# Criss-cross attention on one core: value projection in units of 512 positions instead of 384

## What is computed

```python
q = einsum('oc,bchw->bohw', Wq, x) + bq          # 64 channels, k alike
v = einsum('oc,bchw->bohw', Wv, x) + bv          # 512 channels
energy_H = einsum('bchw,bcgw->bhwg', q, k) - NEG * eye   # along the column of a position
energy_W = einsum('bchw,bchv->bhwv', q, k)               # along its row
att = softmax(concatenate([energy_H, energy_W], -1), -1)
out = gamma * (v summed with att along column and row) + x
```

## Time and profile before

| | |
|---|---|
| median of three runs | 3735.42 us (3734.54 to 3739.78) |
| span of the profiled execution | 3739.5 us (the highest of the three runs is 3739.78 us) |
| PE busy | 3683.0 us, 98% of the span |
| DVE, ACT, POOL busy | 72%, 41%, 17% |
| DMA queue q1 | 869.67 MB, 75.9% of 16 engines |
| PE's share of the chain that ended last | 96% |

### The profile page before, as it was taken

The page is one execution under the profiler, slowest core; times in us unless marked ns, Lnnn a source line. Parts: engine busy times, 40 slices in busy tenths (PEclk is TensorE's granted clock), DMA queues, the critical chain, the costliest instruction groups (busy, mean ns, idle before and its releaser), DMA issues.

```text
span 3739.5 us, 67129 instructions
## 1 busy us (share of the span) xinstructions
PE 3683.0 (98%) x26968; PEld 3663.5 (98%) x26968; DVE 2674.2 (72%) x4324; ACT 1533.3 (41%) x2130; POOL 649.6 (17%) x816
## 2 busy tenths in 40 slices
PE   8799999999999999999999999999999999999999
PEld 7799999999999999999999999999999999999999
DVE  8767787677876778767786677866778657786555
ACT  7523444244442445424454244542444424444111
POOL 1410023100331003210042000420004200042000
PEclk9899999999999999999999999999999999999999
DMA  8687768877698776977769777697776977769665
GB/s 268 178 230 254 254 215 234 245 253 248 203 246 247 240 256 191 259 237 254 247 190 255 242 245 254 196 251 240 259 232 204 250 229 255 230 210 254 204 211 180
DMA packets 333956, 873.97 MB, mean 234 GB/s; under 512 B 34640, under 2 KB 186704, under 8 KB 333648
## 3 DMA queue, kind: packets, MB, share of 16 engines
q1 hardware_dynamic: 333648, 869.67, 75.9%
HBM read 661.92 MB, written 207.62 MB: 233 GB/s over the span
## 4 chain that ended last, share of the span: by engine, by line
PE 96%; DVE 3%; DMA 1%; issue 0%; ACT 0%; SPq 0%; POOL 0%; DVEq 0%; POOLq 0%
PE bank L1044 43%; PE bank L1011 19%; PE bank L1032 18%; PE bank L960 10%; PE bank L972 3%; PE bank L981 3%; DVE E L735 1%; PE bank L996 0%; DVE Sx L714 0%; DVE Sx_first L714 0%; DMA XT_r<-in_x_row 0%; DVE mx_c L730 0%; DVE mx_r L730 0%; DVE zs_c L745 0%; DMA XA_first<-in_x 0%
## 5 line engine op out<-in xcount | busy, mean ns | idle before, releaser
L1044 PE MATMUL bank<-Sy,Wv_hi 128*128 128x384 f32 x6144 | 1595.3, 340 | 8.6 <-DVE Sy L719 8.6
L1044 PEld LDWEIGHTS bank<-Sy,Wv_hi 128*128 128x128 f32 x6144 | 1089.0, 189 | 9.8 <-DVE Y L809 9.8
L1044 PE MATMUL bank<-Sy,Wv_lo 128*128 128x384 f32 x3072 | 1028.5, 335 | 0.0
L809 DVE SCALAR_TENSOR_TENSOR Y<-bank,bv_sb,Y 128x384 f32<-128x384 f32 x768 | 470.3, 612 | 723.9 <-PE bank L1044 723.1
L1032 PE MATMUL bank<-Pt,XT_r 128*128 128x96 f32 x6144 | 719.3, 275 | 3.7 <-DMA XT_r<-in_x_row 3.7
L1032 PEld LDWEIGHTS bank<-Pt,XT_r 128*128 128x128 f32 x6144 | 715.9, 192 | 4.4 <-DMA XT_r<-in_x_row 4.1
L484 POOL TENSOR_TENSOR Pe<-Pe,F 128x384 f32<-128x384 f32 x336 | 286.0, 853 | 2389.5 <-DMA Pe<-e_scratch 2351.0
L617 ACT ACTIVATE Sy<-Y 128x768 fp32r<-128x768 f32 x384 | 319.0, 842 | 793.4 <-PE bank L1044 747.3
L1044 PEld LDWEIGHTS bank<-Sy,Wv_lo 128*128 128x128 f32 x3072 | 577.4, 188 | 0.0
L605 ACT ACTIVATE Y<-bank 128x384 f32<-128x384 f32 x384 | 326.9, 851 | 429.3 <-PE bank L1011 429.3
L793 DVE COPY Y<-bank 128x384 f32<-128x384 f32 x384 | 317.7, 827 | 214.5 <-PE bank L1011 198.0
(11 more groups left out here) (73 smaller groups left out, 3030.2 us busy)
## 6 DMA issues: line engine op xcount, KB each, us to landing
XT_r<-in_x_row SPq DMA_DIRECT2D x384, 384.0 KB, 6.0
Y<-in_x SPq DMA_DIRECT2D x192, 768.0 KB, 5.5
out<-Y SPq DMA_DIRECT2D x184, 768.0 KB, 4.2
XA<-in_x SPq DMA_DIRECT2D x180, 768.0 KB, 6.4
XT_r<-in_x_col SPq DMA_DIRECT2D x192, 384.0 KB, 8.2
XT_c<-in_x_col SPq DMA_DIRECT2D x192, 384.0 KB, 8.0
e_scratch<-E SPq DMA_DIRECT2D x384, 144.0 KB, 3.0
Pe<-e_scratch SPq DMA_DIRECT2D x336, 144.0 KB, 7.6
```

The source lines that it names most:

```text
L809: nc.vector.scalar_tensor_tensor(at, proj_ps[c % 2][:, 0:CP], bv_sb[:, c:c + 1], at, op0=ALU.add, op1=ALU.add).then_inc(out_made, 1)
L1044: last = nc.tensor.matmul(proj_ps[c % 2][:, 0:CP], w[:, ct, at], Sy[:, lo, ct, :], start=(ct == 0 and k == 0), stop=(ct == CT - 1 and k == 2))
```

## The change

Projection no longer follows chunks. The 9216 positions are cut into 18 units of 512 (`UNIT`), each projected with matmuls of 512 columns. A unit covers parts of two chunks, so rounding, `low_y` and `finish` are made in two pieces (`pieces(u)`); three units cover four chunks. After the four slots of a unit PE attends the 5 or 6 image rows of unit u + 2 in one burst (`rows_of`), and 11 rows stand ahead of the first unit where 8 stood. There is a second place for energies behind the slots: slot 4 lies behind the burst's first three rows, slot 5 behind its end. `A_SLOTS` puts three chunks of keys and queries into each of units 5 to 12, `B_SLOTS` the 24 column groups into units 12 to 16. Outputs lie two slots behind the sums (`SPARE`), `Y` has 26 slots, and the last two chunks are stored in quarters. The scratch for software DMA is given as 2048.

```diff
+UNIT = 512
+UNITS = POS // UNIT
+SPARE = 2
+BANKED = CHUNKS - SPARE
+def rows_until(u):
+    return -(-UNIT * (u + 1) // N)
+A_FIRST, A_LAST = 5, 12
+A_SLOTS = {5: (1, 3, 4), **{u: (0, 2, 4) for u in range(6, A_LAST + 1)}}
+B_SLOTS = {12: (5,), **{u: range(6) for u in range(13, 16)}, 16: (0, 1, 2, 3, 4)}
+AFTER_TILES = 4
...
-        Y = sb("Y", [P, CHUNKS + 1, CT, CP])
+        Y = sb("Y", [P, CHUNKS + SPARE, CT, CP])
-        Sy = sb("Sy", [P, 2, CT, CP], F32R)
+        Sy = sb("Sy", [P, 2, CT, UNIT], F32R)
...
             def row_stage(b, more):            # SP
-                load_xtr(b, 3)
+                load_xtr(b, RRING)
+                load_xtr(b, RRING + 1)
                 load_xres(b, 0)
-                load_xtr(b, 4)
-                load_p(b, CHUNKS + 4)
-                load_xtr(b, 5)
+                load_xtr(b, RRING + 2)
+                load_xres(b, 1)
+                load_p(b, CHUNKS + PRING + 1)
+                load_p(b, CHUNKS + PRING + 2)
+                load_freed_xtr(b, 1)
...
+            def round_y(b, u):                 # ACT; low_y and finish on DVE alike
+                act.wait_ge(r_added, past(r_added, b * N + rows_until(u)))
...
+                    for n, lo, at, width in pieces(u):
+                        last = nc.scalar.activation(Sy[:, 0, cts, at:at + width], Y[:, n + SPARE, cts, lo:lo + width], ACT.Copy)
+                    last.then_inc(y_hi_made, 1)
...
+                    def after(slot):           # ACT, row_stage
+                        m, x_next, g = kq(u, slot), split(u, slot), group(u, slot)
+                        if x_next is not None:
+                            round_x(b + 1, x_next, 0)
+                        if m is not None:
+                            evict_kq(b + 1, m)
+                        if x_next is not None:
+                            round_x(b + 1, x_next, 1)
+                        if m is not None:
+                            exponentials(b + 1, m)
+                        if g == 0:
+                            gather_q(b + 1, 0)
+                            gather_q(b + 1, 1)
+                        if g is not None:
+                            if g + 2 < CHUNKS:
+                                gather_q(b + 1, g + 2)
+                            exponentials(b + 1, CHUNKS + g)
+                    for c in range(CT - 1):
+                        after(c)
+                    if group(u, CT - 1) is None:
+                        after(CT - 1)
+                    if u + 1 < UNITS:
+                        round_y(b, u + 1)
+                    if group(u, CT - 1) is not None:
+                        after(CT - 1)
+                    after(AFTER_TILES)
+                    after(AFTER_TILES + 1)
...
+                    for c in range(CT):        # DVE, row_stage
+                        low_x_after(c)
+                        finish(b, u, c)
+                        shift_after(c)
+                        if c and kq(u, c - 1) is not None:
+                            sum_z(b + 1, kq(u, c - 1))
...
+                    rows = rows_of(u + 2)
+                    for h in range(HALVES):
+                        if u + 1 < UNITS:
+                            low_y(b, u + 1, h)
+                        for i in rows[h:h + 1]:
+                            add_row(b, i)
+                    low_x_after(AFTER_TILES)
+                    for i in rows[2:3]:
+                        add_row(b, i)
+                    shift_after(AFTER_TILES)
+                    for i in rows[3:]:
+                        add_row(b, i)
...
-                        last = nc.tensor.matmul(proj_ps[c % 2][:, 0:CP], w[:, ct, at], Sy[:, lo, ct, :],
+                        last = nc.tensor.matmul(proj_ps[c % 2][:, :], w[:, ct, at], Sy[:, lo, ct, :],
...
+                for i in range(rows_until(1)): # PE, row_stage
+                    attend_row(b, i)
...
+                    for c in range(CT):
+                        if kq(u, c) is not None:
+                            project_kq(b + 1, kq(u, c))
+                        project(b, u, c)
+                        energies_after(c)
...
+                    if kq(u, AFTER_TILES) is not None:
+                        project_kq(b + 1, kq(u, AFTER_TILES))
+                    rows = rows_of(u + 2)
+                    for i in rows[:3]:
+                        attend_row(b, i)
+                    energies_after(AFTER_TILES)
+                    for i in rows[3:]:
+                        attend_row(b, i)
+                    energies_after(AFTER_TILES + 1)
```

More of the change, by code:

```diff
@@ L30, with rows_of, turned_for, pieces @@
 COPIES = P // BLOCK
-A_FIRST, A_LAST = 6, 17
-B_FIRST, B_LAST = 18, 22
-B_EACH = 5
-def a_chunks(n):
-    return [2 * (n - A_FIRST), 2 * (n - A_FIRST) + 1] if A_FIRST <= n <= A_LAST else []
-def b_groups(n):
-    first = (n - B_FIRST) * B_EACH
-    return list(range(first, min(first + B_EACH, CHUNKS))) if B_FIRST <= n <= B_LAST else []
+UNIT = 512
[4 more added lines that the diff above has]
+    return -(-UNIT * (u + 1) // N)
+def rows_of(u):
+    return range(rows_until(u - 1), rows_until(u)) if u < UNITS else range(0)
+def turned_for(u):
+    return [i // ROWS for i in rows_of(u) if i % ROWS == 0]
+def pieces(u):
+    at, out = 0, []
+    while at < UNIT:
+        n, lo = divmod(u * UNIT + at, CP)
+        width = min(CP - lo, UNIT - at)
+        out.append((n, lo, at, width))
+        at += width
+    return out
+def first_unit(n):
+    return n * CP // UNIT
+def last_unit(n):
+    return ((n + 1) * CP - 1) // UNIT
+A_FIRST, A_LAST = 5, 12
+A_SLOTS = {5: (1, 3, 4), **{u: (0, 2, 4) for u in range(6, A_LAST + 1)}}
+B_SLOTS = {12: (5,), **{u: range(6) for u in range(13, 16)}, 16: (0, 1, 2, 3, 4)}
+AFTER_TILES = 4
+def kq_chunk(u, slot):
+    slots = A_SLOTS.get(u, ())
+    return (u - A_FIRST) * 3 + slots.index(slot) if slot in slots else None
+def split_chunk(u, slot):
+    if (u, slot) == (A_FIRST - 1, AFTER_TILES):
+        return 0
+    m = kq_chunk(u, slot)
+    return m + 1 if m is not None and m + 1 < CHUNKS else None
+def column_group(u, slot):
+    slots = list(B_SLOTS.get(u, ()))
+    return sum(len(B_SLOTS[v]) for v in B_SLOTS if v < u) + slots.index(slot) if slot in slots else None
 def out_slot(n):
-    return n % (CHUNKS - 1)
+    return n % BANKED
 def criss_cross_attention(nc, x, x_col, x_row, wqk_t, wv_t, bqk, bv, gamma, out):
@@ new lines, in row_stage @@
+                load_p(b, CHUNKS + PRING + 2)
+                load_freed_xtr(b, 1)
+                for u in range(UNITS):
+                    kq, split, group = stage_plan(more)
+                    if kq(u - 1, AFTER_TILES) is not None:
+                        store_row_energies(b + 1, kq(u - 1, AFTER_TILES))
+                    for n in range(CHUNKS):
+                        if first_unit(n) == u + 1:
+                            load_xres(b, n)
+                    if more and u == A_FIRST - 1:
@@ new lines, in row_stage @@
+                    if more and u == UNITS - 1:
+                        load_p(b + 1, PRING)
+                    for c in range(CT):
+                        if split(u, c) is not None and split(u, c) + 2 < CHUNKS:
+                            load_xa(b + 1, split(u, c) + 2)
+                        if kq(u, c) is not None:
+                            store_row_energies(b + 1, kq(u, c))
+                        if c < CT - 1 and group(u, c) is not None:
+                            store_column_energies(b + 1, group(u, c))
+                        if c == 1:
+                            for n in turned_for(u + 2):
+                                if n + PRING < CHUNKS:
+                                    load_p(b, CHUNKS + n + PRING)
@@ L403, in row_stage @@
+                    if u < UNITS - 1:
+                        for n in range(BANKED):
+                            if last_unit(n) == u:
+                                store_out(b, n)
                     else:
@@ L680, in prologue @@
                     if m + 2 < CHUNKS:
-                        round_x(0, m + 2)
+                        for h in range(HALVES):
+                            round_x(0, m + 2, h)
                     if m:
@@ L843, in row_stage @@
                         sum_z(b + 1, 2 * CHUNKS - 2)
-                    finish(b, n, 0)
-                    if more and n + 1 == A_FIRST:
-                        low_x(b + 1, 0)
-                    if b_now and b_now[0]:
-                        sum_z(b + 1, CHUNKS + b_now[0] - 1)
-                    if a_now:
-                        low_x(b + 1, a_now[1])
-                        shift(b + 1, a_now[0])
-                    if b_now:
-                        shift(b + 1, CHUNKS + b_now[0])
@@ new lines, in row_stage @@
+                    if kq(u, CT - 1) is not None:
+                        sum_z(b + 1, kq(u, CT - 1))
+                    rows = rows_of(u + 2)
+                    for h in range(HALVES):
+                        if u + 1 < UNITS:
```

(6 more changed lines are left out.)

395 lines of the change are left out of this document (155 added, 240 removed).

## The result

The changed kernel is slower: 3820.39 us, the median of four runs (3814.38 to 3821.81), against 3737.6 us for the kernel before beside it (3734.54 to 3740.48). The ratio is 1.0221, 95% interval 1.0207 to 1.0236. The profiled execution spans 3820.1 us, 80.6 more than before's 3739.5. The forecast was 3757, so its sign was right, and the size, 21 us against 81, was wrong by a factor of four.

A forecast was written before the change was run, and what follows sets the result against it. PE, busy for 98% of the span, was taken as the bound: 34.8 us saved against waits, clock and stores gave +21 us on 3735.4, so 3757 us; own range 3735 to 3775, 8 in 10 from 3706 to 3788.

The forecast's parts named there:

- rivals 1 (231): Projection matmuls: float32r's extra is paid per column, so only 4.1 us of switches come back; 3787 us, chance 0.20.
- 3 (213): Projection matmuls: weight loading paces those of 384 columns, 512 would hide it, 123 us go; 3664 us, chance 0.05.
- this extra: Float32r matmuls: 13.3 ns over one column a cycle, taken as paid per instruction, so 30.7 us go.
- Rival 2: Handovers: the waits are mostly hidden and the gain per instruction stays; -13 to -30 us, 3714 us, chance 0.25.
- start of the row stage: PE waits for the piece with row 10, 1.7 us six times and 3.6 us twice: 17 us.
- Rival 4: A and B units: DVE becomes the bound, 45 us on top of the forecast; 3802 us, chance 0.03.
- a second price: After unit 17's wait the clock falls to 1.2 GHz: 1.7 us in half of seven batches, 6 us, ends 0 and 20.
- unit 17: From unit 16, PE waits for low_y behind a group's statistics: 1.4 us more in seven batches, 0.6 in the last.
- 2304 fewer float32r matmuls and fewer switches: Projection: 30.7 us from fewer matmuls and 4.1 us from fewer float32-to-float32r switches, a gain of 34.8 us.
- unit 5: PE waits for ACT's evictions before chunk 2's energies, 1.55 us in each of seven batches: 11 us.
- unit 12: PE waits for the first gather before the first column energies, 1.3 us in each of seven batches: 9 us.
- bursts and rows on four banks: In B, six-row bursts can wait for an added row of DVE: 0.3 us in one unit a batch, 2 us.

The follow-up runs named there:

- e1: The changed kernel with PE kept busy in its four places of waiting by 512-column matmuls that nobody reads: 3797.5 us, ratio 1.017.
- run 14: Not a run label: in the text, the first matmuls of a run (consecutive matmuls) make 14 us of the 58 us miss.
- e9: The changed kernel with four moves in its order, and GpSimd's row-stage weight multiplications held until the coming unit's low parts are made: 3740.3 us, ratio 1.0018.
- e10: As e9, with the last tile's two stores at the column stage's start put behind the weights' and XT_c loads: 3737.3 us, ratio 1.0004.

## Why the prediction was wrong

**Right.** The distance: 226.7 ns at 512, the same extra as at 384, so rivals 1 (231) and 3 (213) fell. That this extra is a fixed start-up isn't borne out: between the two widths it is 15.4 to 16.7 ns, and that the two ends agree was luck for the forecast. Rival 2 fell, since nothing hid the waits. The waits came at the four places named, and the experiments took away each by the edit that the reason asks for. At the start of the row stage the size was right in part by luck: the waits ahead of row 8 were not foreseen, and those ahead of row 6 in the last two batches, which the forecast kept, are gone. One reading was wrong without a part in the sum: a float32 product of 384 columns takes 0.64 us for its two records, which is four cycles a column at 2.4 GHz, two for each record. Rival 4, a lag in all A and B units, is not there. Nor would a shift of the medians help: before came out at 3735.4 and 3737.6.

**The step that failed** is the price of the clock, "a second price", which I took as 6 us with 20 as far end. I gave it to unit 17 alone, for half of its seven waits, because before's waits of up to 1.7 us had not brought the clock down. It measured 24 us by the trace and some 20 by e1. In unit 17 the count was right, four spells of 1.6 us; fourteen more followed the waits of units 5 and 12, of the row stage's start and of the column stage, which are shorter (1.4 to 2.4 us), and to which the forecast gave nothing. The earlier trace rows held too few waits of this kind to give a price, and I should have taken it for every wait of over 1.5 us, with "all of them" as an end. It is the largest part of the miss and not the whole: of the 58 us between the two columns below the clock is 18, the first matmuls of a run 14, the bursts 12, the four waits 9 and the column stage 5.

**Terms mis-sized or missing.** From the changed kernel's trace, beside the forecast:

| term | forecast, us | measured, us |
|---|---|---|
| 2304 fewer float32r matmuls and fewer switches | -34.8 | -34.8 by the settled distances, less the next row |
| slower first matmuls of a run of 512 | none | +14 (15.5 - 1.5) |
| unit 17 | 10.6 | 13.8 (22.4 - 8.6) |
| unit 5 | 11 | 11.4 (12.0 - 0.6) |
| unit 12 | 9 | 12.5 (15.3 - 2.8) |
| start of the row stage | 17 | 18.6 (16.5 + 5.8 - 3.7) |
| clock | 6 | 24 |
| bursts and rows on four banks | 2 | some 14, of it some 7 in unit 4's burst |
| column stage, last stores | 0.5 | some 5 |

The measured column sums to some 79, the spans differ by 80.6. The last two rows are differences of distances between the traces; beyond unit 4's burst (e9) no run takes them apart. The single waits were off by 9 us together: in unit 12 I let PE wait 1.3 us where it waited 1.8. The bursts' term missed that `low_y` doubles its time beside GpSimd. That the first matmuls of a run cost more could not be read before, where runs of 384 show nothing of it. It is part of why e10, in which the handovers and the clock are mended, comes out even instead of 30 us ahead: 14 us of the 34.8 are taken back by it. The other 20 us are open. In e10's trace the distances behind the rows' matmuls sum to 1039 us against 1028 before, most of it in waits under 0.8 us, and those of the row energies to 4 us more; this was added up and not tested.

## What to carry to other kernels

Where one engine is busy for 98% of the time, a change that makes its pieces larger must be judged by its handovers: a larger piece takes every engine that prepares it longer, and places without cover (no burst ahead, a queue with one more item) show at once. Add to each wait of 1.5 us or more on TensorE the cost of a fall of the clock as the far end (here 1.6 us; of the 34 waits of over 1.2 us in the changed kernel about half had one), and test that price apart from the wait by matmuls that nobody reads. When a saving per instruction is counted, look at the first instructions of each run as well as at the settled ones.
